# Attention's output product of five head pairs made beside the last two steps, its sums kept on chip

## What is computed

```python
qkv = x @ W_qkv.T                       # x: layer norm of the input, (8, 2048, 1024)
q, k, v = heads(split(qkv))             # 16 heads of 64
weights = softmax(q @ k.T / sqrt(64))   # over all 2048 keys, no mask
out = (weights @ v)                     # heads joined again: (8, 2048, 1024)
out = out @ W_o.T + b_o                 # the output product
x = x + out
```

## Time and profile before

| | us |
|---|---|
| median of 3 runs | 3529.73 (3400.16 to 3662.04) |
| the profiled execution | 3381.05 |
| its span, slowest core (core 3) | 3379.4 |
| its fastest core (core 4) | 3299.0 |
| attention's last two steps and tail on core 3 | 164.8, 82.0, 78.8 |

### The profile page before, as it was taken

The page is one execution under the profiler, slowest core; times in us unless marked ns, Lnnn a source line. Parts: engine busy times, 40 slices in busy tenths (PEclk is TensorE's granted clock), DMA queues, the critical chain, the costliest instruction groups (busy, mean ns, idle before and its releaser), DMA issues.

```text
span 3379.4 us, 39052 instructions; the slowest of 8 cores (3299.0 to 3379.4 us)
## 1 busy us (share of the span) xinstructions
PE 2719.5 (80%) x11770; PEld 1162.0 (34%) x11770; DVE 1984.2 (59%) x2842; ACT 1703.0 (50%) x2015; POOL 382.7 (11%) x437
## 2 busy tenths in 40 slices
PE   1355768799489999999999883678879959889789
PEld 0122223344133444444433331333334424334334
DVE  1477667775557777777765124677777514443433
ACT  2776656563423666666654623666656313414430
POOL 0000102112310001110000100001211211211310
PEclk7676889899798999999965796889989979999999
DMA  7343533233612022220110154122323360000001
GB/s 228 111 122 121 173 123 125 87 96 103 149 19 45 22 39 57 42 39 19 30 35 7 38 148 142 35 83 86 123 83 92 103 212 1 1 20 31 1 7 69
DMA packets 153945, 259.11 MB, mean 77 GB/s; under 512 B 37968, under 2 KB 74064, under 8 KB 153424
## 3 DMA queue, kind: packets, MB, share of 16 engines
q1 hardware_dynamic: 121312, 199.77, 19.4%
q0 software_dynamic: 32432, 56.83, 7.0%
HBM read 220.70 MB, written 52.56 MB: 81 GB/s over the span
## 4 chain that ended last, share of the span: by engine, by line
PE 61%; DVE 14%; ACT 9%; issue 8%; DMA 7%; POOL 1%; SPq 1%; DVEq 0%; ACTq 0%; POOLq 0%
PE fb L1099 11%; PE fb L869 8%; PE aups L1556 8%; PE apps L1670 7%; PE asps L1651 7%; PE mb L2169 6%; PE ajps L1520 3%; DVE fbig L910 2%; PE rs L2060 2%; DVE amx L1567 2%; ACT fbig L905 2%; PE mb L2224 2%; PE mb L1968 1%; DMA xbd<-alnb 1%; DMA fbig<-w1h 1%
## 5 line engine op out<-in xcount | busy, mean ns | idle before, releaser
L1567 DVE TENSOR_REDUCE amx<-aups 128x1 f32<-128x512 f32 x1024 | 662.6, 686 | 253.8 <-PE aups L1556 251.9
L1660 ACT ACTIVATE aet<-asps 128x1024 bf16<-128x1024 f32 x512 | 521.6, 1025 | 294.0 <-PE asps L1651 290.3
L869 PE MATMUL fb<-fxsc,fw1r 128*128 128x512 bf16 x2048 | 561.1, 415 | 96.4 <-DVE fbig L914 66.1
L1099 PE MATMUL fb<-fbig 128*128 128x512 bf16 x2048 | 504.1, 396 | 95.5 <-DVE fbig L839 53.8
L1556 PE MATMUL aups<-ahd 65*128 65x512 bf16 x1024 | 381.0, 415 | 22.1 <-DVE amx L1567 8.5
L1670 PE MATMUL apps<-aet,avt 128*65 128x512 bf16 x1024 | 339.8, 416 | 16.4 <-ACT aet L1660 11.0
L869 PEld LDWEIGHTS fb<-fxsc,fw1r 128*128 128x128 fp8e4 x2048 | 213.3, 105 | 400.6 <-issue 209.3
L1651 PE MATMUL asps<-ahd 65*128 65x512 bf16 x1024 | 340.0, 417 | 0.0
L1099 PEld LDWEIGHTS fb<-fbig 128*128 128x128 fp8e4 x2048 | 204.8, 101 | 362.2 <-issue 143.1
L910 DVE SCALAR_TENSOR_TENSOR fbig<-fb,cw2sb,fbig 128x511 f32<-128x511 f32 x256 | 191.3, 747 | 213.0 <-ACT fbig L905 210.8
L905 ACT ACTIVATE fbig<-fb,cbsb,cw2sb 128x512 f32<-128x512 f32 x256 | 196.3, 770 | 234.4 <-PE fb L869 222.0
(11 more groups left out here) (249 smaller groups left out, 2968.7 us busy)
## 6 DMA issues: line engine op xcount, KB each, us to landing
fw1r<-wq SPq DMA_DIRECT2D x224, 128.0 KB, 2.1
fbig<-wq SPq DMA_DIRECT2D x112, 256.0 KB, 2.7
fbig<-w1h SPq DMA_DIRECT2D x32, 512.0 KB, 12.9
fw2f<-w2h SPq DMA_DIRECT2D x64, 256.0 KB, 3.1
fbig<-w2h SPq DMA_DIRECT2D x28, 512.0 KB, 3.9
fxq<-x SPq DMA_DIRECT2D x8, 1024.0 KB, 9.0
fbig<-x POOLq DMA_DIRECT2D x32, 256.0 KB, 5.6
xa<-fbig POOLq DMA_DIRECT2D x32, 256.0 KB, 3.7
```

What stands on the lines that cost most here:

```text
L869: tp = T(lambda e, dc=dc: e.matmul(bank[b][:, :], sl[:, o + dc * 128:o + (dc + 1) * 128], xr[:, dc * 512:(dc + 1) * 512], start=(dc == 0), ...
L1099: tp = T(lambda e, j=j: e.matmul(bank[2 + j][:, :], w2r[s][:, o + j * 128:o + (j + 1) * 128], xi2[:, hc * 512:(hc + 1) * 512], start=(hc = ...
L1567: lambda e, hh=hh, c=c: e.tensor_reduce(m[:, c:c + 1], ups[hh][:, :], axis=AX.X, op=ALU.max),
L1660: ta = A(lambda e: e.activation(et[g % 3][:, :], sps[s][:, :], AF.Exp, scale=0.125), wait=[tp, tk.get(("ef", g % 3))])
```

## The change

- The eight products per output are split: head pairs 0 to 4 (EA = 5) are now made by a generator `g_wo` through the single bank ajps, pulled two matmuls per group in step 6 from group 12 on, and one per group in step 7; what is left is drained at the end of step 7 (with 104 + 64 pulls for 160 matmuls nothing is).
- Behind the fifth matmul of each output, DVE adds product, bias and residual in f32 into the residual's tile (`scalar_tensor_tensor`), which stays on chip. There are now 32 such tiles: the 8 on lnb, 16 on the layer norm's xln, 4 on qkb, 4 on wqk.
- All 32 residual loads are issued on SP's queue at the end of step 5, behind the end of projection 7 and of the transfers that used qkb. The wo loads are issued there too, instead of at the end of step 6.
- The tail makes the last three matmuls of each output (ec = 5, 6, 7; the first two of the first eight outputs before norm 7), adds them to the tile with `tensor_tensor`, and stores. The bias is no longer added there, and no load or buffer stands in its way.

```diff
@@ -1359,7 +1359,15 @@
                 m_sb = lnb[:, 2048:2560]
                 r_sb = lnb[:, 2560:3072]
                 v_sb = lnb[:, 3072:3584]
-                res = [lnb[:, i * 512:(i + 1) * 512] for i in range(8)]
+
+
+                res = [lnb[:, i * 512:(i + 1) * 512] for i in range(8)] + \
+                    [xln[:, i * 1024:(i + 1) * 1024].bitcast(F32)
+                     for i in range(16)] + \
+                    [qkb[:, i * 1024:(i + 1) * 1024].bitcast(F32)
+                     for i in range(4)] + \
+                    [wqk[i // 2][:, (i % 2) * 1024:(i % 2 + 1) * 1024]
+                     .bitcast(F32) for i in range(4)]
 
                 qp = qkb[:, 0:T]
                 kp = qkb[:, T:2 * T]
@@ -1376,7 +1384,7 @@
                 s_ao = [dsem("aao") for _ in range(2)]
                 s_dn = [dsem("adn") for _ in range(2)]
                 s_wo = dsem("awo")
-                s_res = [dsem("ares") for _ in range(8)]
+                s_res = [dsem("ares") for _ in range(32)]
 
                 def dget(sem, dst, src, wait=(), eng="sync"):
                     return em.go(eng, lambda e: e.dma_start(dst, src),
@@ -1728,6 +1736,41 @@
                     after(18 if t < 7 else 5, inv)
 
 
+                EA = 5
+                idx = [(qb, dc) for qb in range(4) for dc in range(DC)]
+                rl = {}
+
+                def res_load(n):
+                    qb, dc = idx[n]
+                    rl[n] = dget(s_res[n], res[n],
+                                 x_src[dc * 128:(dc + 1) * 128,
+                                       qb * QT:(qb + 1) * QT],
+                                 wait=[tk["r"], tk["proj", 7], tk["65", 7]])
+
+                def wo_mm(out, n, ec, first, last, wait):
+                    qb, dc = idx[n]
+                    return P(lambda e: e.matmul(
+                        out, wo[:, ec * D + dc * 128:
+                                ec * D + (dc + 1) * 128],
+                        ao[:, ec * T + qb * 512:ec * T + (qb + 1) * 512],
+                        start=(ec == first), stop=(ec == last)),
+                        wait=wait, mark=(ec == last))
+
+                def g_wo():
+                    for n, (qb, dc) in enumerate(idx):
+                        for ec in range(EA):
+                            tp = wo_mm(jps[:, :], n, ec, 0, EA - 1,
+                                       [tk["wo"], tk["norm", ec]] +
+                                       ([tk["jf"]] if ec == 0 else []))
+                            if ec < EA - 1:
+                                yield
+                        t = V(lambda e, n=n, dc=dc: e.scalar_tensor_tensor(
+                            res[n], jps[:, :], bo_sb[:, dc:dc + 1], res[n],
+                            ALU.add, ALU.add), wait=[tp, rl[n]])
+                        tk["jf"] = tk["res", n] = t
+                        yield
+
+
                 def pull(g, n=1):
                     for _ in range(n):
                         next(g, None)
@@ -1761,7 +1804,10 @@
                     if t < 7:
                         precast(t)
                     u = g_pass1(t + 1) if t + 1 < 8 else iter(())
-                    p = g_proj(t + 2) if t + 2 < 8 else iter(())
+                    if t + 2 < 8:
+                        p = g_proj(t + 2)
+                    elif t == 6:
+                        p = g_wo()
                     while later and t == 0 and ("nm", 0, 1) not in tk:
                         tick()
                     scores(t, 0)
@@ -1771,19 +1817,28 @@
                         pull(u, 2)
                         values(t, g, 0)
                         values(t, g, 1)
-                        pull(p, 2 if g % 8 == 0 else 1)
+                        if t < 6:
+                            pull(p, 2 if g % 8 == 0 else 1)
+                        elif t == 7 or g >= 12:
+                            pull(p, 2 if t == 6 else 1)
                         tick()
                     pull(u)
-                    pull(p)
+                    if t < 6:
+                        pull(p)
                     tick()
                     tick()
-                    if t == 6:
+                    if t == 7:
+                        for _ in p:
+                            pass
+                    if t == 5:
                         for ec in range(DC):
                             tk["wo"] = dget(
                                 s_wo, wo[:, ec * D:(ec + 1) * D],
                                 woT.ap()[ec * 128:(ec + 1) * 128, :],
                                 wait=[tk["pv", 5]],
                                 eng="gpsimd")
+                        for n in range(32):
+                            res_load(n)
                 while later:
                     tick()
 
@@ -1793,49 +1848,30 @@
                          ups[0][:, :], ups[1][:, :], jps[:, :]]
                 rt = [tk["sf", 0, 0], None, tk["sf", 1, 0], None, tk["pf"],
                       tk["u0f"], tk["u1f"], tk["jf"]]
-                idx = [(qb, dc) for qb in range(4) for dc in range(DC)]
-                rl = {}
-
-                def res_load(n):
-                    qb, dc = idx[n]
-                    i = n % 8
-                    rl[n] = dget(s_res[i], res[i],
-                                 x_src[dc * 128:(dc + 1) * 128,
-                                       qb * QT:(qb + 1) * QT],
-                                 wait=[tk.get(("st", i)), tk["r"]])
-                for n in range(4):
-                    res_load(n)
-                def wo_mm(n, ecs):
-                    qb, dc = idx[n]
+
+                def wo_rest(n, ecs):
                     i = n % 8
                     for ec in ecs:
-                        tp = P(lambda e, ec=ec: e.matmul(
-                            rings[i], wo[:, ec * D + dc * 128:
-                                         ec * D + (dc + 1) * 128],
-                            ao[:, ec * T + qb * 512:
-                               ec * T + (qb + 1) * 512],
-                            start=(ec == 0), stop=(ec == DC - 1)),
-                            wait=[tk["wo"], tk["norm", ec]] +
-                            ([rt[i]] if ec == 0 else []),
-                            mark=(ec == DC - 1))
+                        tp = wo_mm(rings[i], n, ec, ecs0, DC - 1,
+                                   [tk["norm", ec]] +
+                                   ([rt[i]] if ec == ecs0 else []))
                     return tp
 
+                ecs0 = EA
 
                 for n in range(8):
-                    wo_mm(n, range(DC - 1))
+                    wo_rest(n, range(ecs0, DC - 1))
                 for n, (qb, dc) in enumerate(idx):
                     i = n % 8
-                    if n + 4 < 32:
-                        res_load(n + 4)
-                    tp = wo_mm(n, range(DC) if n >= 8 else [DC - 1])
-                    t = V(lambda e, i=i, dc=dc: e.scalar_tensor_tensor(
-                        res[i], rings[i], bo_sb[:, dc:dc + 1], res[i],
-                        ALU.add, ALU.add), wait=[tp, rl[n]])
+                    tp = wo_rest(n, range(ecs0, DC) if n >= 8
+                                 else [DC - 1])
+                    t = V(lambda e, i=i, n=n: e.tensor_tensor(
+                        res[n], rings[i], res[n], ALU.add),
+                        wait=[tp, tk["res", n]])
                     rt[i] = t
-                    tk["st", i] = dget(s_res[i],
-                                       x_dst[dc * 128:(dc + 1) * 128,
-                                             qb * QT:(qb + 1) * QT],
-                                       res[i], wait=[t])
+                    dget(s_res[n], x_dst[dc * 128:(dc + 1) * 128,
+                                         qb * QT:(qb + 1) * QT],
+                         res[n], wait=[t])
 
         def layer1(x_src, x_dst):
             barrier()
```

## The result

The changed kernel takes 3344.61 us, median of 4 runs (3342.46 to 3348.92); the profiled execution is 3342.97, its span 3341.4. Beside the kernel before the ratio is 0.9846, 95% interval 0.9822 to 0.987: about 52 us less, a clear gain, though under 2%.

What follows compares the result with a forecast made beforehand. PE at the low clock in step 6 was taken as the bound. Core 3: step 6 -15, step 7 +3, tail -37, 3330; core 5 last at 3338, so -42, 3488 from the median; likeliest 3465 to 3505, ends 3320 and 3620.

Steps and rivals of the forecast that it cites:

- What bounds the kernel: Attention step 6: PE busy 163.3 of 164.8 us at 1.2 GHz; the slow core is the one longest there.
- The clock recovers from group 12 on: Step 6: 2 dense matmuls in 8 bring the clock back in some 10 us.
- The rival of a clock that stays low: Step 6 all at 427 ns per matmul: 221 us, +56 on core 3, total +22, 3552; chance 0.11.
- Step 6: Second half of attention: 150 us on core 3 (-15), 148 on a core that had 130 (+18).
- a fast core's wait for wo: Step 6, group 12: a core arriving at +19 waits about 12 us for wo, which drops its clock.
- The clock's term: Step 6: +4 us for recovery, once after the start and once at the middle, 8 in all.
- Step 7: 56 added matmuls cost +6, the low clock at its start goes, -3: 85 us, +3.
- Tail: After step 7: loads and five eighths of the product leave, stores take 24 us: 41.5 us against 78.8, -37.
- The sum on the profiled execution: Whole kernel: core 5 becomes the slowest at 3338; the profiled run, 3381, becomes 3339.
- Against 3379.4: -42: Whole kernel: new slowest core 5 at 3338 set against core 3's old end at 3379.4, -42 us, 1.2%.
- I subtract 42 from the median: 3488: Forecast time: the median shown, 3529.7, less the 42 us gain, gives 3488.
- within 2%: Whole kernel: result within about 2%, 70 us, put as what a measurement can tell from no change; chance 0.69.

Runs made afterwards that it cites:

- dense1: Kernel before plus one unused 128x128 by 128x512 matmul per group of step 6 (64 in all): 3332.0 us, ratio 0.9822.
- thin1: Kernel before plus the same number of unused matmuls in step 6, but with 65 rows (65x128 by 65x512): 3412.0 us, one execution, no ratio.
- resheld: Changed kernel with all 32 residual loads held on SP's queue until wo has landed: two executions, 3339.3 and 3343.7 us, no ratio.
- tailres: Changed kernel without early matmuls: residuals and wo loaded early, all eight products of each output in the tail; ratio 0.9944 against the kernel before.
- only7: Changed kernel with no early matmul in step 6, all 160 pulled in step 7; ratio 0.9969 against the kernel before.
- reslate: Changed kernel with 28 of the 32 residual loads emitted at group 16 of step 6; ratio 0.9892 against the kernel before.

## Why the prediction was right, and where it was wrong

*What bounds the kernel: right.* PE at the lower level in step 6, on the core where that lasts longest. dense1 and thin1 show it by two kernels that differ only in 64 unused matmuls, in their rows and in what they read.

*The clock recovers from group 12 on: right.* On every core of the changed kernel, including those that fell at the start. My reason, more full matmuls per group than in the steps that recover, was only an analogy before; dense1 against thin1 shows that full matmuls bring it back. They aren't the only way: cores 0 and 7 of the changed kernel fell at the start and were back within 8 to 13 us, before any full matmul was made, as core 4 of before did at its middle. But in thin1 and on the other seven cores of before it stayed low up to the step's end. The rival of a clock that stays low is out. The Trainium skill's sentence (TensorE: Matmul & The Clock Gate, What's actually happening), that activity releases the throttle, holds only if activity isn't read as PE being busy: thin1 was busy for 99.7% of 191 us and stayed at 0.51.

*Step 6: size.* I had 150 on a low core and 148 on the other; measured 145.4 on core 3, and 140.5 and 140.9 on cores 2 and 4, which kept full clock up to the wait for wo. The group at full clock came out as said: 66.9 / 32 = 2.1 us, with eleven stalls of up to 1.3 us, and a fast core's wait for wo of 10.9 us on core 2 and 9.2 on core 4 (12 expected). The clock's term was too large: at the middle I had 4 us for a fall on every core, and three of eight had one, of some 1.5 us. The cause I gave for wo's lateness, the residual loads beside it, stands (resheld). *Step 7:* 85 expected, 85.9. *Tail:* 41.5 expected, 42.5 to 46.7 on the eight cores; from the first store to the end it was 27.7 us on core 3 and 28.8 on core 7, where I had 24 + 1.5. I took the rate of a stretch of 4 us, 349 GB/s, for all 8.4 MB; over the whole stretch core 3 moved 305 GB/s.

*The sum on the profiled execution: right by 4 us, in part by luck.* 3339 expected, 3343 measured. Core 7 and not core 5 is last: which core enters step 6 latest differs from execution to execution. It entered at 1730.5 us (1736.2 expected), its step 6 took 143.3 (148), step 7 and tail 3 us more than expected, and from attention's end to its own it needed 1337.9 us where I had 1327. So -6, -5, +3 and +11 nearly cancel. Why the part behind attention took longer than on core 5 before stays open; on other cores before it was up to 1337.

*The size against before: too small.* -42 expected, -52 measured (44 to 60 by the interval; 46 against the 17 executions of before beside the experiments). As far as the record shows, not a price but the base was off. I compared a latest core, entering at 1736, with an execution in which that core kept its clock for half of step 6 (core 5, 130 us). Were that core to fall at the start, it would end at 1736.2 + 165 + 82 + 79 + 1330 = 3392, and 15 of the 17 executions lie at 3385 to 3396; the profiled one, 3381, is lower than all but one of them. The step that failed here is "Against 3379.4: -42". With such a core on both sides it is 3392 - 3339 = -53. That a late core falls in most executions is argued from these times, since of before there is one trace; in those of tailres and only7, where step 6 has the same work on PE, the last core is a low one (cores 4 and 7).

*The number on record: wrong by 143 us.* This is the step that failed most: "I subtract 42 from the median: 3488". The median of 3400, 3530 and 3662 stood 4.4% above the profiled execution, and I carried these 149 us into the changed kernel as if they were part of it. What the runs showed in its place is 3342 to 3349 us for the changed kernel and 3395 to 3400 for the one before. My low end, 3320, came from the lowest run and the high end, 3620, from the highest; that 3345 lies inside is owed to this width, and the likeliest range, 3465 to 3505, misses it by 120. The profiled run was the better base.

*The chances.* A measurement can tell less than the 2% that I put as its limit: its interval here is 0.5% wide, and excludes no change. I gave 0.69 to "within 2%", which is where it fell, but read as "no change" that was wrong; the sum itself said 1.2% faster, and 1.5% was measured.

*What I hadn't seen* is that the early products don't pay as built. I priced 104 matmuls with coupling and stalls at 109 - 52 x 1.56 = 28 us and never set this beside the 0.216 us that each costs in the tail, 22 us for the 104. It was in the rows: in step 6 PE was busy 163.3 of 164.8 us and had no idle time to give.

## What to carry to other kernels

Before work is moved beside a busy step, price it in both places: here, beside a step that its own engine bounds, it cost what it did in the tail, plus the coupling. Where an engine's granted clock is low in a stretch and full beside it, compare what the two stretches run before anything is optimised there; here 64 matmuls with an unused result were worth at least as much as the rewrite. When the slowest of several cores sets the time, build the base from what the slowest usually is, step by step, and not from the one profiled execution, nor from a median of a few scattered runs.

## What the runs showed of the hardware that I had not expected

- With 64 matmuls of 128x128 by 512 among 384 others, all of these with 65 rows or 65 columns of weights, the clock fell at the step's start but came back within about 5 us (22 on one core of eight), and was 0.97 and 1.00 in the two halves of a step that got 0.51 without them; with 64 of 65x128 by 512 it stayed at 0.51 (dense1, thin1). The step went from 165 to 108 and to 191 us.
- The queue that only issues transfers ran ahead of the compute: loads emitted 16 groups later started with the first ones (reslate).
- The slowest of eight weight loads of 256 KB landed at 21.6 to 26.2 us beside 8.4 MB of other loads and at 9.1 to 14.5 with these held back (resheld). The transfers of one queue slowed those of the other.
